# Reordered pairs, an earlier third softmax, stores by tile and sums zeroed by GpSimd in a four-layer graph network on one core

## The chip, the cores and the metric

The kernel runs on one core of one Trainium2 chip, as one program. The metric is the time of one execution in microseconds (us), as the device reports it. Beside it stands one execution taken by the hardware profiler, whose trace tells what each engine did: PE is the matrix engine, DVE the vector engine, ACT the scalar engine, POOL is GpSimd, SP the engine that here only issues transfers.

## The reference

The graph has 3125 nodes with rows of 256 numbers, and 53125 edges (50000 drawn ones and one loop per node), sorted by destination. Four layers follow each other, each with a residual and a layer norm. Cut to what matters:

```python
x = layernorm(x + gat_two_heads(x))        # e = exp(-leaky_relu(s_l[src] + s_r[dst])), sums over src
x = layernorm(x + gru(sum_over_edges(x[src] + rel[type]), x))
x = layernorm(x + poincare(x))             # below
x = layernorm(x + conv(relu(conv(x, edge_attr)), edge_attr))   # two TransformerConv, 4 heads
# poincare:
h = dir(x @ W.T + b) * magnitude
scores = h[src] @ a_s + h[dst] @ a_t
ex = exp(scores - segment_max(scores, dst)[dst]);  w = ex / (segment_sum(ex, dst)[dst] + 1e-10)
hc = h + segment_sum(h[src] * w, dst)
p = tanh(|hc|) * hc / |hc|, cut to length 0.95
# conv:
alpha = (q[dst] * (k[src] + e)).sum / 8, softmax over dst; out = segment_sum((v[src] + e) * alpha, dst) + x @ Ws + bs
```

## The kernel before, in words

Nodes lie in 25 tiles of 128 (`NT`), treated in 5 groups of 5 tiles (`NG`, `GRP`). Edges lie in 440 tiles of 128 (`ET`): 220 pairs, 55 groups of 8 tiles (`NH`, `HB`), 28 batches of 16 tiles (`NBT`, `NB`). The phases run one after the other, with a barrier of all engines between them: `start_up` (integers of the edges, first projection), `aggregate0` and `finish0` (first layer), `aggregate1` and `finish1` (second), `project2`, `aggregate2` and `finish2` (third, and the projections q, k, v, skip of the first conv), `attend(1)`, `between` (end of the first conv and the projections of the second), `attend(2)`, `last_rows`.

All aggregations work alike. POOL gathers the 128 source rows of a tile by an indirect transfer into a ring of slots (40 in the third layer). ACT weighs the rows, and PE multiplies them by a one-hot matrix (`oh`, written by DVE for 8 tiles at a time) into one of 4 windows in PSUM. DVE adds the window to the block of `acc` to which the tile's destinations belong. `acc` holds 128x6800 numbers and is zeroed by a DVE instruction at the head of each aggregation.

The third and fourth layers need a softmax over edges that share a destination. `RunningSoftmax` does it for a batch of 16 tiles in parts 0 to 7 (`sm.pe`, `sm.dve`, `sm.act`): the scores are turned by PE, DVE runs a running maximum along them, small transposes carry the values at tile ends across (`ends`, `car`, `firsts`, `back`), ACT takes the exponential, and PE turns the weights back (`w_in`). The parts are a chain: each waits for the one before, on another engine. In `aggregate2` a slot of the program is a batch: step j of 8 holds part j of the softmax of batch b-1, the scatter of pair j of batch b-2 on PE, and its windows' additions on DVE. So a pair is scattered 16 pairs after its scores. In `attend` the order is written by pairs p = 0, 1, ...: two parts of the softmax per pair in the first four pairs of every eight, none in the next four, and the scatter 12 pairs behind (`LAG`). Engines take their instructions strictly in the order written; POOL may refill a slot once the scatter of its old rows is done (`products`).

`finish2` has these chains per group of 5 tiles: DVE `combine(i)` writes hc; ACT squares it and takes the root of the sums; DVE `squash` asks ACT for a tanh (`t_ask`), works through twelve small instructions, five on rows and the moments; ACT takes a root; DVE `norm`; ACT writes the group's rows of `X`. Then PE transposes each tile, ACT copies it (`take_turned`), PE multiplies by the 256x1024 weights, and DVE takes the products (`take`, 4 instructions). `store` writes a whole group's k, v and skip rows by two transfers; the phase ends when all have landed. `between` has the same projection behind `rest(i)`, which ends the first conv, and `last_rows` writes the output.

Of the kernel before, what the change touches and what calls it, by code (L numbers as in the profile page):

```python
# [60 lines left out]
def graph_layers(nc, a, out):  # L61
    ctx = ExitStack()
    with ctx:
# [115 lines left out]
        def start_up():  # L179
# [6 lines left out]
            with ExitStack() as scope:  # L186
# [28 lines left out]
                with nc.Block() as block:  # L215
# [29 lines left out]
                    def _(pool):  # L245
# [8 lines left out]
                        nc.gpsimd.memset(ones[:, :], 1.0).then_inc(consts, 1)  # L254
                        pool.wait_ge(starts_ready, 1)
# [194 lines left out]
        def aggregate0():  # L450
            names = "lo_in0 lo_in1 lo_in2 lo_in3 oht_ready oh_ready z_terms z_ready w_ready rows_ready products added zeroed dve act".split()
            lo_in0, lo_in1, lo_in2, lo_in3, oht_ready, oh_ready, z_terms, z_ready, w_ready, rows_ready, products, added, zeroed, dv, ac = [
# [11 lines left out]
            with ExitStack() as scope:  # L464
# [5 lines left out]
                with nc.Block() as block:  # L470
# [45 lines left out]
                    def _(dve):  # L516
# [59 lines left out]
                        nc.vector.memset(acc[:, :, :], 0.0).then_inc(zeroed, 1)  # L576
# [3 lines left out]
                        dve.wait_ge(zeroed, 1)  # L580
# [48 lines left out]
        def finish0():  # L629
# [3 lines left out]
            with ExitStack() as scope:  # L633
# [4 lines left out]
                wprod = held(scope, "wprod2", [P, 2, F])  # L638
                rows = held(scope, "rows_f0", [P, 3, GRP, F])
                low = held(scope, "low_f0", [P, 2, GRP, F])  # L640
                with nc.Block() as block:
                    @block.vector
                    def _(dve):
# [31 lines left out]
                        dve.wait_ge(wt_taken, 10)  # L675
                        dve.wait_ge(ld_x, 16 * 8)
                        for n in range(2):
                            step(nc.vector.tensor_tensor(wprod[:, :, :], w2T[:, :, 0:F], bc_a2[:, n, :].unsqueeze(1).broadcast_to([P, 2, F]), ALU.mult))
                            step(nc.vector.tensor_reduce(w2T[:, :, F + 1 + n:F + 2 + n].rearrange("p k a -> p (k a)"), wprod[:, :, :], AX, ALU.add))
                            step(nc.vector.tensor_tensor(wprod[:, 0, :], bc_b2[:, 0:F], bc_a2[:, n, :], ALU.mult))  # L680
                            step(nc.vector.tensor_reduce(bc_b2[:, F + 1 + n:F + 2 + n], wprod[:, 0, :], AX, ALU.add))
                        step(nc.vector.tensor_tensor(bc_t[:, 0:512], bc_t[:, 0:512], bc_b[:, 0:512], ALU.add))
# [70 lines left out]
        def aggregate1():  # L753
            a_in = [sem(f"a1_a_in{u}") for u in range(2)]
            aT_out = [sem(f"a1_aT_out{u}") for u in range(2)]
            names = "oh_ready products added zeroed at_ready at_taken fix_in fix_out".split()
# [386 lines left out]
        def tiles_of(b):  # L1143
            return max(0, min(NB, ET - b * NB)) if 0 <= b < NBT else 0
# [353 lines left out]
        def finish2():  # L1498
            h_ready, n_ready, t_ask, t_ready, var_ready, std_ready, f_ready, x_ready, x_out, dv, ac = [
                sem("f2_" + n) for n in "h_ready n_ready t_ask t_ready var_ready std_ready f_ready x_ready x_out dve act".split()]  # L1500
            with ExitStack() as scope:
# [4 lines left out]
                with nc.Block() as block:  # L1506
                    @block.vector
                    def _(dve):
# [508 lines left out]
```

## Time and profile before

| | us |
|---|---|
| three timed runs | 4553.05, 4554.0, 4560.82 |
| median | 4554.0 |
| the profiled execution | 4529.55 |
| its span, first to last instruction | 4527.8 |
| PE busy in the span | 3176.2 (70%) |
| DVE busy | 2951.7 (65%) |
| POOL busy | 2749.4 (61%) |
| ACT busy | 1634.9 (36%) |

The profiled execution is 24.45 us below the median of the timed ones. Busy time is time with an instruction of the engine under way; no engine is near 100%, since each phase has another limit. The mean granted clock of PE is 0.806 of full speed. POOL's time is nearly all that of issuing indirect transfers.

### The profile page before, as it was taken

The numbers are of one execution on the slowest core, as the hardware profiler recorded it, in microseconds if no ns is written. First come the engines' busy times: TensorE is split into PE (matmuls) and PEld (weight loads), VectorE is DVE, ScalarE is ACT, GpSimd is POOL, SyncE is SP. The second block draws the span as 40 slices with busy tenths as digits, with TensorE's granted clock in tenths as the row PEclk, the third lists the DMA queues.
The fourth block names the chain that finished last, engine by engine and source line by source line (L and its number), as shares of the span: only waits on it lengthen the run. The fifth ranks groups of instructions, "written<-read, shape, count | busy, mean of one in ns | idle before, by whom it ended". The sixth has DMA issues, their size and how long they took to land. (4 is left out here: it accounts for less than half of the span.)

```text
span 4527.8 us, 51805 instructions
## 1 busy us (share of the span) xinstructions
PE 3176.2 (70%) x11623; PEld 2181.9 (48%) x11623; DVE 2951.7 (65%) x7240; ACT 1634.9 (36%) x4707; POOL 2749.4 (61%) x2215
## 2 busy tenths in 40 slices
PE   4555553476666853777775788888887878888884
PEld 3444442344444442444443356666564456666662
DVE  3445447344444464666665478888887578888887
ACT  3334444011111221223233245555552145555553
POOL 4666661766665005667760188888881288888881
PEclk7667776688887875556667889999998999999996
DMA  4544443566566203444441599999994599999993
GB/s 134 112 113 111 114 112 84 154 195 198 184 192 183 87 12 116 114 114 113 114 99 52 145 188 192 190 186 191 190 181 107 162 185 192 190 190 186 191 179 85
DMA packets 378970, 660.99 MB, mean 146 GB/s; under 512 B 59010, under 2 KB 161395, under 8 KB 378676
## 3 DMA queue, kind: packets, MB, share of 16 engines
q0 software_dynamic: 190208, 406.78, 47.5%
q1 hardware_dynamic: 184356, 247.08, 17.0%
q10 hardware_dynamic: 4112, 3.83, 0.3%
q8 instruction: 110, 1.80, 0.2%
q14 instruction: 184, 1.51, 0.1%
HBM read 582.15 MB, written 75.33 MB: 145 GB/s over the span
## 5 line engine op out<-in xcount | busy, mean ns | idle before, releaser
L1653 POOL DMA_INDIRECT t_kv<-kv_tab,srcT x880 | 1415.7, 1609 | 648.8 <-ACT t_kv L1779 389.4
L1280 POOL DMA_INDIRECT grow<-h_tab,srcT x440 | 451.2, 1025 | 468.3 <-POOLq L83 276.7
L776 POOL DMA_INDIRECT grow<-x_tab,srcT x440 | 441.1, 1003 | 304.2 <-issue 107.1
L1836 PE MATMUL bank<-t_kv,t_oh 128*128 128x260 f32 x1760 | 555.4, 418 | 99.8 <-DVE acc L1730 66.6
L476 POOL DMA_INDIRECT grow<-h_tab,srcT x440 | 436.2, 991 | 245.2 <-issue 96.6
L1809 PE MATMUL bank<-we,t_aT 128*128 128x256 f32 x1760 | 504.7, 413 | 26.2 <-DMA t_aT<-attrT_tab 25.5
L1820 PE MATMUL bank<-H,t_ohT 128*128 x1760 | 497.4, 409 | 23.0 <-DVE t_ks L1690 22.3
L1778 ACT COPY t_kv<-bank 128x512 f32<-128x512 f32 x440 | 256.3, 582 | 618.6 <-PE bank L1809 583.7
L1796 ACT ACTIVATE t_kv<-t_kv 128x64 f32<-128x64 f32 x1760 | 465.8, 344 | 13.4 <-DVE t_kv L1706 13.4
L824 DVE TENSOR_TENSOR acc<-acc,bank 128x272 f32 x440 | 192.5, 437 | 393.9 <-PE bank L901 151.3
L1836 PEld LDWEIGHTS bank<-t_kv,t_oh 128*128 128x128 f32 x1760 | 318.2, 201 | 258.5 <-ACT t_kv L1796 133.5
L1730 DVE TENSOR_TENSOR acc<-acc,bank 128x260 f32 x880 | 368.6, 419 | 98.3 <-DVE acc L1730 71.2
L1408 PE MATMUL bank<-grow,oh 128*128 128x257 f32 x880 | 393.8, 601 | 35.0 <-DVE acc L1337 16.1
L1820 PEld LDWEIGHTS bank<-H,t_ohT 128*128 128x128 f32 x1760 | 361.4, 207 | 88.3 <-issue 31.4
L901 PE MATMUL bank<-grow,oh 128*128 128x272 f32 x880 | 296.6, 462 | 121.9 <-issue 98.1
L1809 PEld LDWEIGHTS bank<-we,t_aT 128*128 128x128 f32 x1760 | 335.0, 200 | 81.6 <-DMA t_aT<-attrT_tab 27.2
L548 DVE TENSOR_TENSOR acc<-acc,bank 128x258 f32 x440 | 186.6, 424 | 274.7 <-PE bank L626 108.7
L626 PE MATMUL bank<-grow,oh 128*128 128x258 f32 x880 | 319.5, 535 | 37.0 <-issue 27.9
L1690 DVE TENSOR_TENSOR t_ks<-t_kv,bank 128x512 f32<-128x512 f32 x440 | 298.9, 679 | 68.8 <-DMA t_kv<-kv_tab,srcT 61.3
L1337 DVE TENSOR_TENSOR acc<-acc,bank 128x257 f32 x440 | 184.2, 419 | 192.4 <-PE bank L1408 135.1
L849 ACT COPY aT<-bank 128x512 f32<-128x512 f32 x110 | 64.1, 585 | 620.3 <-PE bank L874 285.7
L1408 PEld LDWEIGHTS bank<-grow,oh 128*128 128x128 f32 x880 | 236.9, 294 | 101.8 <-issue 41.7
(396 smaller groups left out, 4804.5 us busy)
## 6 DMA issues: line engine op xcount, KB each, us to landing
t_aT<-attrT_tab SPq DMA_DIRECT2D x110, 512.0 KB
lob<-lo_tab SPq DMA_DIRECT2D x110, 256.0 KB
arow<-in_edge_attr SPq DMA_DIRECT2D x440, 64.0 KB
attrT_tab<-aT SPq DMA_DIRECT2D x55, 512.0 KB
t_lob<-lo_tab SPq DMA_DIRECT2D x110, 256.0 KB
grow<-h_tab,srcT POOLq DMA_INDIRECT x880
t_kv<-kv_tab,srcT POOLq DMA_INDIRECT x880
kv_tab<-kv SPq DMA_DIRECT2D x10, 1290.0 KB, 5.2
```

The source lines that it names most:

```text
L476: nc.gpsimd.indirect_dma_start(out=grow[:, t % RA, :], out_offset=None, in_=h_tab, in_offset=bass.IndirectOffsetOnAxis(ap=srcT[:, t:t + 1] ...
L626: nc.tensor.matmul(PS[t % WIN][:, 0:F + 2], oh[:, g % 2, u, :], grow[:, t % RA, :], start=True, stop=True).then_inc(products, 1)
L776: nc.gpsimd.indirect_dma_start(out=grow[:, t % RA, 0:F], out_offset=None, in_=x_tab, in_offset=bass.IndirectOffsetOnAxis(ap=srcT[:, t:t + ...
L1280: nc.gpsimd.indirect_dma_start(out=grow[:, t % R2, :], out_offset=None, in_=h2_tab, in_offset=bass.IndirectOffsetOnAxis(ap=srcT[:, t:t + 1 ...
L1408: nc.tensor.matmul(PS[2 + t % WIN2][:, 0:F + 1], oh[:, t // HB % 2, t % HB, :], grow[:, t % R2, 0:F + 1], start=True, stop=True).then_inc( ...
L1653: nc.gpsimd.indirect_dma_start(out=kv[:, t % UB, :], out_offset=None, in_=kv_tab, in_offset=bass.IndirectOffsetOnAxis(ap=srcT[:, t:t + 1], ...
L1690: nc.vector.tensor_tensor(ks[:, p % 2, :, :], kv[:, s:s + 2, 0:F], PS[2 + p % 2][:, :].rearrange("p (v f) -> p v f", v=2), ALU.mult).then_ ...
L1730: nc.vector.tensor_tensor(window, window, PS[4 + t % WIN3][:, 0:LHW], ALU.add).then_inc(added, 1)
L1796: last = nc.scalar.activation(part, part, ACT.Copy, scale=u_rows[:, t % UB, h, C3:C3 + 1])
L1809: mm = nc.tensor.matmul(PS[p % 2][:, v * F:(v + 1) * F], aT[:, g % 3, u * P:(u + 1) * P], we[:, :], start=True, stop=True)
L1820: mm = nc.tensor.matmul(PS[2 + p % 2][:, v * F:(v + 1) * F], ohT[:, g % 2, u * P:(u + 1) * P], H[:, ds(blocks[u], 1), :].rearrange("p b f ...
L1836: nc.tensor.matmul(PS[4 + t % WIN3][:, 0:LHW], oh[:, t // HB % 2, t % HB, :], kv[:, t % UB, F:KVW], start=True, stop=True).then_inc(produc ...
```

## The change

The change has eight parts.

1. Zeroing `acc`. The DVE memset at the head of all five aggregations is gone. POOL zeroes the whole of it in `start_up`, and in `finish0`, `finish1`, `finish2` and `between` it zeroes each group's part (128x1360) once DVE has read it.
2. The score weights of the third layer (`wprod`, 8 instructions) go from the end of `finish0` to groups 10 and 12 of `aggregate1`; the addition to `bc_t` goes to the head of `aggregate1`.
3. `aggregate2` is written by pairs like `attend`: `LAG` 12, two parts of the softmax in each of the first four pairs of eight.
4. In both, the last batch's softmax is begun at pair 220 (`softmax_at`), in `attend` four pairs earlier than before, in `aggregate2` likewise as soon as its scores are there.
5. The last group's rows of the projections are stored tile by tile (`store_tiles`); the memset in `begin` covers only the columns that need it.
6. `finish2` puts `combine` and the squares of two groups ahead, and the chain of group i directly before that of i+1; the weights' `begin` comes one group later.
7. `between` puts `rest(i + 1)` behind the second `take` of group i.
8. `last_rows` stores the last group by tiles.

```diff
@@ start_up, POOL
                         nc.gpsimd.memset(ones[:, :], 1.0).then_inc(consts, 1)
+                        nc.gpsimd.memset(acc[:, :, :], 0.0)
@@ finish0, finish1, finish2, between: a POOL program like this one
+                            pool.wait_ge(h_ready, i + 1)
+                            nc.gpsimd.memset(group(acc, i), 0.0).then_inc(acc_zero, 1)
@@ aggregate2
+        LAG = 12
+        def softmax_at(p):
+            b, k = (p // 8 - 1, p % 8) if p < PAIRS else (NBT - 1, p - PAIRS)
+            return (b, k) if b >= 0 and k < 4 else None
@@ aggregate2, DVE
-                        nc.vector.memset(acc[:, :, :], 0.0)
...
-                        for b in range(NSLOT):
...
+                        for p in range(STEPS):
+                            q, batch = p - LAG, softmax_at(p)
+                            if batch:
+                                sm.dve(dve, step, batch[0], 2 * batch[1])
...
+                            if batch:
+                                sm.dve(dve, step, batch[0], 2 * batch[1] + 1)
+                                if batch[1] == 3:
+                                    take_weights(batch[0])
@@ Projection
+            def store_tiles(self, sp, i, tab):
+                for t in range(i * GRP, (i + 1) * GRP):
+                    sp.wait_ge(self.mm_taken, 2 * (t + 1))
+                    sp.dma_start(kv_tab[t * P:(t + 1) * P, :], self.kv[:, i % 2, t % GRP, :]).then_inc(self.out_done[i % 2], 16)
+                    sp.dma_start(tab[t * P:(t + 1) * P, :], self.skip[:, i % 2, t % GRP, :]).then_inc(self.out_done[i % 2], 16)
@@ finish2, DVE
+                        combine(0)
+                        combine(1)
                         for i in range(NG + 2):
                             if i < NG:
-                                combine(i)
-                            if i == 0:
-                                pr.begin(dve, step)
+                                squash(i)
                             takes(i - 2, 0, 2)
-                            if 1 <= i <= NG:
-                                squash(i - 1)
-                            takes(i - 2, 2, 3)
-                            if 1 <= i <= NG:
-                                norm(i - 1)
-                            takes(i - 2, 3, GRP)
+                            if i < NG:
+                                norm(i)
+                            if i + 2 < NG:
+                                combine(i + 2)
+                            if i == 1:
+                                pr.begin(dve, step)
+                            takes(i - 2, 2, GRP)
@@ between, DVE
-                            if i + 1 < NG:
-                                rest(i + 1)
                             add_bias(i)
-                            for t in range(i * GRP, (i + 1) * GRP):
-                                pr.take(dve, t)
+                            for n in range(GRP):
+                                pr.take(dve, i * GRP + n)
+                                if n == 1 and i + 1 < NG:
+                                    rest(i + 1)
```

PE in the middle of `aggregate2` before, from the end of one batch to the first four parts of the next softmax. L1408 is the scatter (two rows are a pair), L1185, L1188 and L1191 are the turned scores, the ends and the carried values of the softmax:

```order
L1408 MATMUL bank<-grow,oh 128x257 x4
L1185 MATMUL bank<-ident,s_al 16x128
L1408 MATMUL bank<-grow,oh 128x257 x2
L1188 MATMUL bank<-ident,s_run 1x16
L1408 MATMUL bank<-grow,oh 128x257 x2
L1191 MATMUL bank<-ident,s_rowC 16x1
L148 TENSOR_LOAD rows_i
```

The same place after; the scatter is now L1426, and the softmax L1205 to L1217:

```order
L1426 MATMUL bank<-grow,oh 128x257 x4
L1205 MATMUL bank<-ident,s_al 16x128
L1208 MATMUL bank<-ident,s_run 1x16
L1426 MATMUL bank<-grow,oh 128x257 x2
L1211 MATMUL bank<-ident,s_rowC 16x1
L1214 MATMUL bank<-ident,s_tot 1x16
L1426 MATMUL bank<-grow,oh 128x257 x2
L1217 MATMUL bank<-ident,s_rowC 16x1
L148 TENSOR_LOAD rows_i
```

Two small transposes that wait for each other through DVE now stand next to each other, with no scatter between, and the four pairs behind them have none.

ACT in `finish2` before, from the norm of group 1 on. L1578 and L1580 are the squares and their root, L1585 the tanh, L1588 the deviation's root, L1592 the rows of `X`, L1467 the copies of transposed tiles:

```order
L1580 ACTIVATE small<-ss 128x5
L1585 ACT_TABLE_LOAD
L1585 ACTIVATE small<-small 128x5
L1588 ACT_TABLE_LOAD
L1588 ACTIVATE small<-small 128x5
L1592 ACTIVATE X<-hc,small 128x256 x5
L1467 COPY xT<-bank 128x256 x2
L1578 ACTIVATE sq,ss<-hc 128x256 x5
L1580 ACTIVATE small<-ss 128x5
L1467 COPY xT<-bank 128x256
```

After, from the rows of `X` of group 0 on (L1610 and L1612 are the squares and root, L1620 the tanh, L1624 the deviation's root, L1629 `X`, L1492 the copies):

```order
L1629 ACTIVATE X<-hc,small 128x256 x5
L1610 ACTIVATE sq,ss<-hc 128x256 x5
L1612 ACTIVATE small<-ss 128x5
L1620 ACT_TABLE_LOAD
L1620 ACTIVATE small<-small 128x5
L1624 ACT_TABLE_LOAD
L1624 ACTIVATE small<-small 128x5
L1629 ACTIVATE X<-hc,small 128x256 x5
L1610 ACTIVATE sq,ss<-hc 128x256 x5
L1612 ACTIVATE small<-ss 128x5
L1492 COPY xT<-bank 128x256 x2
```

The first copies of transposed tiles, for which PE's first products wait, stood directly behind the first `X`; they now stand behind the second `X` and one more group of squares.

## Rows read from the trace of the kernel before

**Rows 1.** Windows of three phases: us, busy and count by engine, PEclk, DMA share, GB/s.
```profile
1728.00:2412.00 684.00, 476.39 (x1600) 307.05 (x1600) 414.28 (x1281) 193.24 (x496) 450.54 (x440) 0.61 0.41 107
2412.00:2572.00 160.00, 102.54 (x250) 46.19 (x250) 82.64 (x280) 48.63 (x126) 0.00 (x0) 0.82 0.27 95
2572.00:3468.00 896.00, 732.74 (x2920) 535.75 (x2920) 763.81 (x1804) 458.69 (x1377) 708.02 (x440) 0.94 0.97 179
```

**Rows 2.** The gathers of aggregate2 by source line: ns min/median/max; idle us, times.
```profile
L1280 POOL DMA_INDIRECT grow<-h_tab,srcT x440: 940/946/2226, 1727.4 to 2369.2; - x147
...
  issue: 109.5, 348
  PE bank L1408: 73.4, 84
```

**Rows 3.** PE groups of aggregate2: busy us, mean ns, idle before by releaser.
```profile
L1408 PE MATMUL bank<-grow,oh 128*128 128x257 f32 x880 | 393.8, 601 | 35.0 <-DVE acc L1337 16.1 <-ACT grow L1377 11.0 <-issue 7.6
```

**Rows 4.** Timeline of aggregate2: start us, us, engine, line, [idle before <-releaser].
```profile
1749.69 0.17 DVE L1313 TENSOR_TENSOR s_al<-s_al,grow 128x8 f32<-128x8 f32 x1 [7.87 <-DMA grow<-h_tab,srcT]
...
1773.79 0.16 DVE L1321 COPY s_fm<-bank 128x1 f32<-128x1 f32 x1 [11.88 <-remote]
...
2349.69 0.14 DVE L1230 COPY s_carry<-bank 16x1 f32<-16x1 f32 x1
...
2350.93 0.41 DVE L1235 TENSOR_TENSOR_SCAN s_tot<-contn,s_T 16x128 f32<-16x128 bf16 x1
...
2351.50 2.08 PE L1408 MATMUL bank<-grow,oh 128*128 128x257 f32 x4
...
2372.44 1.11 PE L1408 MATMUL bank<-grow,oh 128*128 128x257 f32 x4
...
2376.38 0.17 DVE L1313 TENSOR_TENSOR s_al<-s_al,grow 128x8 f32<-128x8 f32 x1
...
2410.56 0.42 DVE L1337 TENSOR_TENSOR acc<-acc,bank 128x257 f32 x1 [0.21 <-DVE acc L1337]
```

**Rows 5.** Timeline at the head of aggregate2, DVE.
```profile
1728.19 5.72 DVE L1339 MEMSET acc<- 128x6800 f32 x1 [5.44 <-issue]
...
1741.04 0.17 DVE L1313 TENSOR_TENSOR s_al<-s_al,grow 128x8 f32<-128x8 f32 x1 [4.88 <-DMA grow<-h_tab,srcT]
```

**Rows 6.** Timeline of finish2: ACT, then PE and DVE.
```profile
2417.85 0.21 ACT L1580 ACTIVATE small<-ss 128x5 f32<-128x5 f32 x1
...
2431.36 0.21 ACT L1585 ACTIVATE small<-small 128x5 f32<-128x5 f32 x1
...
2437.86 0.21 ACT L1588 ACTIVATE small<-small 128x5 f32<-128x5 f32 x1 [4.99 <-DVE small L427]
...
2442.39 5.25 PE L1459 MATMUL bank<-wq,xT 128*128 128x512 f32 x8
...
2445.96 0.42 DVE L1484 SCALAR_TENSOR_TENSOR H<-bank,b_all 128x256 f32<-128x256 f32 x1 [5.07 <-PE bank L1459]
...
2449.62 0.43 DVE L1484 SCALAR_TENSOR_TENSOR H<-bank,b_all 128x256 f32<-128x256 f32 x1 [1.18 <-PE bank L1459]
...
2462.99 0.69 PE L1448 MATMUL bank<-ident,X 128*128 128x128 f32 x2 [4.38 <-ACT X L1592]
```

**Rows 7.** Timeline at the ends of finish2 and last_rows: last takes, next phase, last store.
```profile
2561.72 0.41 DVE L1490 TENSOR_TENSOR skip<-bank,b_all 128x256 f32<-128x256 f32 x1
...
2570.41 0.35 SPq L1662 DMA_DIRECT2D t_aT<-attrT_tab  x1
...
4521.37 0.41 SPq L1953 DMA_DIRECT2D out_nodes<-H  x1
```

**Rows 8.** Timeline of DVE in start_up and at the end of finish0.
```profile
4.39 0.38 DVE L274 TENSOR_SCALAR blk_of_edge_i<-I 128x420 int32<-128x420 int32 x1 [1.49 <-DMA I<-in_dst]
...
785.88 0.69 DVE L678 TENSOR_TENSOR wprod<-w2T,bc_a 128x512 f32<-128x512 f32 x1
...
790.60 0.69 DVE L682 TENSOR_TENSOR bc_t<-bc_t,bc_b 128x512 f32<-128x512 f32 x1
```

More of the change, by code:

```diff
@@ L928, in finish1, with _ @@
                 u_rows = held(scope, "u_f1", [P, GRP, F])
+                acc_zero = sem("f1_acc_zero")
                 with nc.Block() as block:
+                    @block.gpsimd
+                    def _(pool):
+                        for i in range(NG):
+                            pool.wait_ge(xt_ready, (i + 1) * GRP)
+                            nc.gpsimd.memset(group(acc, i), 0.0).then_inc(acc_zero, 1)
                     @block.sync
@@ new lines, in _ @@
+                        for p in range(STEPS):
+                            q, batch = p - LAG, softmax_at(p)
+                            if batch:
+                                sm.pe(pe, batch[0], 2 * batch[1], sums_done, min(NH, 2 * batch[0] + 2))
+                            if p % 4 == 2 and p // 4 < NH:
+                                terms(p // 4)
+                            if batch:
+                                sm.pe(pe, batch[0], 2 * batch[1] + 1, sums_done, 0)
+                            if 0 <= q < PAIRS:
+                                for t in range(2 * q, 2 * q + 2):
+                                    if t % HB == 0:
+                                        pe.wait_ge(oh_ready, t // HB + 1)
+                                    pe.wait_ge(rows_ready, t + 1)
+                                    if t >= WIN2:
+                                        pe.wait_ge(added, t - WIN2 + 1)
+                                    nc.tensor.matmul(PS[2 + t % WIN2][:, 0:F + 1], oh[:, t // HB % 2, t % HB, :], grow[:, t % R2, 0:F + 1],
+                                                     start=True, stop=True).then_inc(products, 1)
@@ L1505, in finish2, with _ @@
                 pr = Projection(scope, 1, X, None)
+                acc_zero = sem("f2_acc_zero")
                 with nc.Block() as block:
+                    @block.gpsimd
+                    def _(pool):
+                        for i in range(NG):
+                            pool.wait_ge(h_ready, i + 1)
+                            nc.gpsimd.memset(group(acc, i), 0.0).then_inc(acc_zero, 1)
                     @block.vector
@@ L1572, in copies, with squares @@
                                 pr.take_turned(act, t)
+                        def squares(i):
+                            act.wait_ge(h_ready, i + 1)
+                            for n in range(GRP):
+                                last = nc.scalar.activation(sq[:, n, :], hc[:, i % 3, n, :], ACT.Square, accum_out=ss[:, i % 3, n:n + 1])
+                            step(last)
+                            nc.scalar.activation(small[:, i % 3, 4, :], ss[:, i % 3, :], ACT.Sqrt).then_inc(n_ready, 1)
@@ L1580, in _ @@
[L1580 to L1592 removed]
+                                act.wait_ge(t_ask, i + 1)
@@ L1875, in between, with _ @@
                 pr = Projection(scope, 2, H, xr)
+                acc_zero = sem("b_acc_zero")
                 with nc.Block() as block:
+                    @block.gpsimd
+                    def _(pool):
+                        for i in range(NG):
+                            pool.wait_ge(h_ready, i + 1)
+                            nc.gpsimd.memset(group(acc, i), 0.0).then_inc(acc_zero, 1)
                     @block.sync
```

245 lines of the change are left out of this document (111 added, 134 removed).

## The prediction

> **What bounds the kernel now.** I read the page first. No engine is near its limit over the whole span, so the question is asked phase by phase, with a window each [rows 1]. In `attend` the DMA engines are busy 0.97 of the time at a PE clock of 0.94, for 896 us: whatever is taken off DVE there is behind transfers. In `aggregate2` (684 us) nobody is full: PE 476 of 684, DVE 414, POOL 451, DMA 0.41, and PE's granted clock is 0.61, so it is most of the time at its lower level of 1.2 GHz. In `finish2` (160 us) PE is busy 102.5, and idle for the rest.
>
> For `aggregate2` I then read who waits. POOL's shortest path is its gathers: 0.95 us each, and 0.31 (109.5/348) between two that wait for nothing; 73.4 us went by waiting for PE to free a ring slot [rows 2]. So the order of PE's work holds POOL up. The first batch of 16 tiles is scored at 1749.7 and the last, half a batch, at 2376.4 [rows 4]: 626.7 us over 26.5 batches, **23.65 us a batch**. POOL alone would need 16 x 1.26 = 20.2. Of PE, a pair of scatters is 1.11 us at its higher clock and 2.08 at its lower [rows 4]. The group's sum, 393.8 us over 220 pairs, is 1.79 a pair [rows 3], which lies between.
>
> In `finish2` the chain of group 0 runs 24.5 us from the root at 2417.9 to PE's first product at 2442.4; tiles then follow at a pitch of 2449.62 - 2445.96 = 3.66 us, until PE has to wait for the next group's `X`, 4.38 us at 2463.0 [rows 6]. From 2442.4 to the last take at 2562.1 it is 119.7 us [rows 6, 7], where the first tile's 5.25 and 24 x 3.66 would be 93.1.
>
> **`aggregate2`, new order.** The half of a batch with the softmax (four pairs) and the free half are costed apart. Softmax half on PE, at the low clock: 4 x 2.08 = 8.3 for scatters. All that PE does besides scatters in this window is 476.4 - 393.8 = 82.6 us [rows 1, 3], 3.0 a batch, of which the half has the larger part, 2.2. Then the waits of transposes that now stand side by side. The worst is from `car` to `tot`: DVE's chain from 2349.69 to 2351.34 [rows 4] is 1.65, and with the way there and back some 2.2; the two before and behind it I put at 1.1 each, by the length of their shorter chains on DVE. Sum 8.3 + 2.2 + 4.4 = **14.9**. Free half: at the low clock PE would need 8.3 + 0.8 = 9.1; at the high one 4.4 + 0.6, and DVE becomes the bound with 8 additions at a pitch of 0.42 + 0.21 = 0.63 [rows 4], 5.0, and some 2.1 for one-hots, places and scores (DVE's 414 us of work [rows 1] are 15 a batch, of which additions 6.7, softmax about 4.7, and the rest 3.6 is halved): 7.1. So a batch costs between 14.9 + 7.1 = 22.0 and 14.9 + 9.1 = 24.0. I take 22.1, since PE had pairs of 1.11 us in a third of the time already, and the free half lets it run without gaps. That is 1.55 x 26.5 = 41 us. Bounds: if PE were at the high clock throughout, POOL's 16 x (1.025 busy [451/440, rows 1] + 0.31) = 21.3 is next, a gain of 62; at the low clock throughout and with waits a little longer (24.3), a loss of 17.
>
> The tail: from the last scores, 2376.4, to the last addition's end, 2411.0, it is 34.6 us [rows 4]. The new tail has one softmax half (14.9, without terms 14), then 8 pairs at DVE's pitch of 2 x 0.63 = 1.27 (10.2) and some 5 for last waits: 29, so **5** gained (0 to 9). The ring: a slot comes free 12 instead of 16 pairs after its scores, so POOL's lead grows by 8 tiles; this takes the 73.4 us of waiting away and is in the 22.1 already.
>
> **`finish2`.** New chain from the squares on: root of group 0 at 2418.1 as now; squares of group 1 end 2.2 later, 2420.3; the tanh with its table 1.6 later; from tanh to the deviation's root 2437.86 - 2431.36 = 6.5 [rows 6], 2428.4; `X` of group 0 done at 2431.5. Squares(2) to 2433.8, tanh(1) 2435.3, root 2441.8, `X` of group 1 at 2444.9, squares(3) 2447.2, and only now the first copies: PE starts at **2447.7**, 5.3 later than now. But then two groups of `X` lie ready, and each further group (about 13.4 us of ACT and DVE chain) is due within 18.3 us (5 x 3.66) of PE's: PE runs without gaps, 93.1 us, to 2540.8, plus 1.2 for the last take, 2542. Against 2562.1 that is 20 (15, if one stall of 4.4 stays, to 21).
>
> **Stores by tile.** From the last take to the next phase's first transfer it is 2570.41 - 2562.13 = 8.3 us, for 1.98 MB [rows 7]. The output's last group, 0.6 MB, needs 6.4 from its issue to the span's end. By these two a MB costs 1.4 us and one tile (0.40 MB) 6.1; a steeper slope cannot be excluded, with a fixed part of 3.5 it would be 4.5. Gain 2.2 to 3.8, taken **3** in `finish2` and **3** in `between`; for `last_rows` 0.5 to 2.5, taken 1.
>
> **Zeroing.** At the head of `aggregate2` DVE's 5.72 us end at 1733.9, and its first scores wait another 4.88 us, until 1741.0, for a gather [rows 5]: worth 0 there, and as the gathers start with the phase in every aggregation, in all five. On POOL, 20 memsets of a group are at DVE's speed 5.72/5 = 1.14 us each, in phases where POOL has no gather [rows 1]: 0 if hidden, 23 if each delayed DVE by its length; taken 1 lost. In `start_up` the whole memset starts at about 2.1 and ends at 7.8; DVE wants to begin at 4.39 [rows 8]. Lost between 0 and 3.4, and more if POOL is slower than DVE; taken **3**.
>
> The Trainium skill, "SBUF — State Buffer", section "Who interferes with whom", says that a DVE instruction in a two-port mode and a GpSimd instruction exclude each other for the whole instruction, and one with at most one SBUF input outside such modes doesn't contend. No row of the trace shows such an overlap. By that rule the start would lose the 3.4, and the group memsets only what meets a copy or a scalar operation.
>
> **The rest.** In `attend` the last batch's softmax begins four pairs earlier; DMA ends the phase at 0.97, and in the tail DVE and PE have room: 1.5 each, together 3 (0 to 6). `finish0` sheds nine DVE instructions, 785.88 to 791.29, 5.4 us [rows 8], but the store of `x_tab` issued just ahead has to land: 2 (0 to 5). They come back in `aggregate1`, twice 2.2 us between additions, where DVE has idle time: 0 (-4 to +4). `rest(i + 1)` behind the takes in `between`: 0.
>
> Sum: 41 + 5 + 20 + 3 + 3 + 1 + 3 + 2 - 3 - 1 = **74**. The profiled execution would go from 4529.6 to 4456 and the median, 24 above it, from 4554 to **4480**.
>
> **Rivals.** (A) *The clock stays low in `aggregate2`.* For it: 0.61 now, and waits added in the softmax half. 24.3 us a batch is 17 lost instead of 41 gained: 4480 + 58 = 4538. With 24.0 it is 4530. Against: PE's idle gaps in the free half go. Chance 0.15. (B) *Slower than before.* At 1773.79 DVE waited 11.88 us [rows 4] for something that the profile doesn't name, while POOL filled the ring at its full rate. In the new order POOL is never held, so such stalls could recur all along; in one of every four batches they cost 7 x 12 = 84 us and cancel the 74 with the 9 us more that 0.2% is. From 7 on the kernel is slower; 10 would give 4600. Against: in `attend` POOL is busy 708 of 896 us and PE as much [rows 1] without such gaps. Chance 0.05.
>
> The Trainium skill, "Runtime: NRT & Kernel Launch", section "Instruction fetch mechanics", says that instructions are fetched in sequence and mostly hidden, and that a taken branch can stall an engine. By this rule such a stall belongs to a phase's head and would not recur; B would then be worth nothing.
>
> (C) *POOL's own pace is reached*: 21.3 a batch, 21 us more gained, 4459. For it: DVE and PE both have room at the high clock. Chance 0.14. (D) *GpSimd's memsets shut DVE out* in all phases: 22 more lost, 4502. It decides nothing alone. Chance 0.04. (E) *Nothing measurable*: A together with stalls left in `finish2`, or a first gather later by what POOL has before it; 4546 to 4563. Chance 0.04.
>
> **How the numbers follow.** The main case has 0.58 and gives 4480; its own range, from the bounds of its terms taken two or three at a time, is 4462 to 4504. The range for all reaches to C below and A above: **4448 to 4538**, which leaves out B, E and the edges of A, some 1.5 in 10. 0.2% is 9 us, about what this measurement can tell from no change. Main, A, C and D are faster by more (0.91, less 0.02 for A at its worst); B is slower 0.05, E gives the same 0.04 and the rest of A 0.02. So 0.89, 0.06, 0.05.
>
> **What would show it.** In the profile after: `aggregate2` some 640 us with a granted clock above 0.61, POOL's waits for PE nearly gone, batches 22 us apart; `finish2` about 137 us, its first product later by 5 us and no wait of PE for `X`; 5 us from the last take to the next phase; in `start_up` DVE's first instruction on the integers at 7.8. The forecast is wrong if a batch takes 24 us, at a clock of 0.55, or if each second pair in the softmax half waits longer than 2.2.

## The result, and the profile after

The changed kernel takes 4540.5 us (median of 9 runs, 4520.3 to 4544.9) where the kernel before takes 4553.1 (9 runs on the same chip, 4546.9 to 4566.9): ratio **0.9967**, 95% interval 0.9952 to 0.9981. It is faster, by 13 us by the medians and 15 by the ratio, and not by 74. The predicted 4480 was missed, and the range of 4448 to 4538 too, by 2.5 us. The profiled execution is, against that, 13 us longer than the one before (span 4540.9 against 4527.8). Two single profiles 0.3% apart don't decide on the whole, but they show where the stages moved.

The first view has the windows, one each for `aggregate2`, `finish2`, `attend(1)` and `between` (columns as in [rows 1]):

```profile
1739.00:2453.00 714.00, 445.59 (x1600) 302.45 (x1600) 415.60 (x1279) 194.38 (x497) 439.76 (x440) 0.63 0.39 102
2453.00:2587.00 134.00, 94.70 (x250) 43.53 (x250) 80.86 (x279) 48.78 (x126) 6.24 (x5) 0.84 0.32 112
2587.00:3487.00 900.00, 737.46 (x2920) 538.39 (x2920) 757.76 (x1806) 458.59 (x1377) 710.72 (x440) 0.93 0.97 178
3487.00:3598.00 111.00, 94.87 (x250) 43.45 (x250) 66.46 (x154) 9.32 (x25) 6.16 (x5) 0.93 0.49 165
```

`finish2` fell from 158.6 to 134 us, as forecast. `aggregate2`, which was to give 46 us, grew from 685 to 714, with a granted clock that did rise (0.61 to 0.63) and PE 31 us less busy. The gathers of that phase by source line, to be set beside [rows 2]:

```profile
L1300 POOL DMA_INDIRECT grow<-h_tab,srcT x440: 940/946/1733, 1739.6 to 2405.3; - x147
...
  PE bank L1426: 104.5, 88
  issue: 102.8, 323
```

POOL waits longer for PE than before (104.5 us after 73.4), in spite of the eight slots more of lead. Of each of these waits (84 before, 88 now) 0.30 us is the pause that stands between any two gathers. One batch in the timeline of that trace (start us, us, engine, line; the scatter is L1426, the turned scores L1205, the turned weights L1223):

```profile
1898.30 0.28 PE L1205 MATMUL bank<-ident,s_al 128*16 128x128 f32 x1 [2.50 <-DVE s_al L1333]
...
1901.49 0.17 PE L1211 MATMUL bank<-ident,s_rowC 1*16 1x1 f32 x1
1901.89 0.15 DVE L1250 COPY s_carry<-bank 16x1 f32<-16x1 f32 x1 [0.90 <-PE bank L1211]
...
1905.90 0.17 PE L1217 MATMUL bank<-ident,s_rowC 1*16 1x1 f32 x1
1908.26 0.15 DVE L1272 COPY s_carry<-bank 16x1 f32<-16x1 f32 x1 [2.41 <-DMA flags<-f_tab]
...
1910.02 2.08 PE L1426 MATMUL bank<-grow,oh 128*128 128x257 f32 x4 [2.12 <-issue]
...
1912.91 0.26 PE L1223 MATMUL bank<-ident,s_d 16*128 16x16 f32 x1
...
1914.47 0.42 DVE L1357 TENSOR_TENSOR acc<-acc,bank 128x257 f32 x1 [1.03 <-PE bank L1426]
...
1916.17 0.43 DVE L1349 TENSOR_TENSOR acc<-acc,s_fm 128x257 f32 x1 [0.42 <-issue]
...
1922.70 0.28 PE L1205 MATMUL bank<-ident,s_al 128*16 128x128 f32 x1 [2.52 <-DVE s_al L1333]
```

The batch takes 24.4 us: 14.6 with the softmax, to the turned weights, and 9.8 without. DVE gets the second carried value (L1272) 2.36 us after the start of the transpose that makes it (L1217), a transpose of 16 numbers; over the batches the mean of this is 1.3 us. Over batches 4 to 24 the mean period is 24.4 us, worked out from the starts of L1205: 14.1 to the turned weights and 10.3 behind them.

`finish2` went by its forecast steps. Its ACT and PE rows after, beside [rows 6], with the last take and the next phase's first transfer, beside [rows 7]:

```profile
2462.71 0.21 ACT L1620 ACTIVATE small<-small 128x5 f32<-128x5 f32 x1
2469.21 0.21 ACT L1624 ACTIVATE small<-small 128x5 f32<-128x5 f32 x1 [4.99 <-DVE small L428]
...
2487.74 0.21 ACT L1612 ACTIVATE small<-ss 128x5 f32<-128x5 f32 x1
2488.35 6.11 PE L1484 MATMUL bank<-wq,xT 128*128 128x512 f32 x8 [14.74 <-ACT xT L1492]
...
2494.51 3.60 PE L1484 MATMUL bank<-wq,xT 128*128 128x512 f32 x8
...
2582.32 0.41 DVE L1515 TENSOR_TENSOR skip<-bank,b_all 128x256 f32<-128x256 f32 x1
...
2587.40 0.34 SPq L1697 DMA_DIRECT2D t_aT<-attrT_tab  x1
```

The tanh-to-root chain is 6.5 us again; PE starts 35.4 us into the stage instead of 30.5 (4.9 later, forecast 5.3) and needs 94.4 us to the last take (forecast 94.3). From there it is 4.7 us to the next transfer where it was 8.3.

### The profile page after: what moved, and what is told of

Its sections match the earlier page's. It is cut to its first block and busy times, and to the rows that moved or that the text cites. A ratio compares the mean times of both kernels' runs of the same rounds, so it can differ in the third digit from the quotient of the medians.

```text
span 4540.9 us, 51843 instructions
## 1 busy us (share of the span) xinstructions
PE 3139.2 (69%) x11623; PEld 2176.7 (48%) x11623; DVE 2928.8 (64%) x7235; ACT 1634.8 (36%) x4707; POOL 2766.9 (61%) x2236
## 5 line engine op out<-in xcount | busy, mean ns | idle before, releaser
L1300 POOL DMA_INDIRECT grow<-h_tab,srcT x440 | 439.8, 999 | 313.4 <-PE bank L1426 104.5
L477 POOL DMA_INDIRECT grow<-h_tab,srcT x440 | 432.2, 982 | 256.7 <-issue 95.4
L822 DVE TENSOR_TENSOR acc<-acc,bank 128x272 f32 x440 | 192.5, 438 | 405.1 <-PE bank L907 180.2
L1426 PE MATMUL bank<-grow,oh 128*128 128x257 f32 x880 | 359.8, 566 | 54.7 <-ACT grow L1397 32.5
L907 PE MATMUL bank<-grow,oh 128*128 128x272 f32 x880 | 299.1, 467 | 98.7 <-issue 62.5
L625 PEld LDWEIGHTS bank<-grow,oh 128*128 128x128 f32 x880 | 233.4, 275 | 107.7 <-issue 41.8
L1426 PEld LDWEIGHTS bank<-grow,oh 128*128 128x128 f32 x880 | 228.3, 279 | 111.1 <-issue 47.5
```

What stands on the lines that cost most here:

```text
L477: nc.gpsimd.indirect_dma_start(out=grow[:, t % RA, :], out_offset=None, in_=h_tab, in_offset=bass.IndirectOffsetOnAxis(ap=srcT[:, t:t + 1] ...
L625: nc.tensor.matmul(PS[t % WIN][:, 0:F + 2], oh[:, g % 2, u, :], grow[:, t % RA, :], start=True, stop=True).then_inc(products, 1)
L907: nc.tensor.matmul(PS[t % WIN1][:, 0:AC], oh[:, g % 2, u, :], grow[:, t % RA, :], start=True, stop=True).then_inc(products, 1)
L1300: nc.gpsimd.indirect_dma_start(out=grow[:, t % R2, :], out_offset=None, in_=h2_tab, in_offset=bass.IndirectOffsetOnAxis(ap=srcT[:, t:t + 1 ...
L1426: nc.tensor.matmul(PS[2 + t % WIN2][:, 0:F + 1], oh[:, t // HB % 2, t % HB, :], grow[:, t % R2, 0:F + 1], start=True, stop=True).then_inc( ...
```

## The experiments

Each ran beside the kernel before on one chip. The chips were of two kinds: on four of them the kernel before takes 4302 to 4309 us, here the faster kind; three times, the first measurement among them, it took 4522 to 4554, the slower kind. The first two traces are of the slower kind. Each chip was used in one sitting only, so "kind" is a name for what was seen: whether it belongs to the chip for good is not shown. A stage's length is that in the one profiled execution of its run.

**1. The old order of `aggregate2` in the changed kernel.** The phase is that of before, without DVE's memset.

```diff
-                        for p in range(STEPS):
-                            q, batch = p - LAG, softmax_at(p)
+                        for b in range(NSLOT):
+                            c = b - 2
+                            for j in range(8):
```

> The changed kernel with one part undone: aggregate2 has the order of before (a batch's softmax over eight pairs, scatter 16 pairs behind), without the memset on DVE. Theory 1, read from the trace after: the new order made aggregate2 longer, 24.4 us a batch instead of 23.4, because its two halves are bound in turn by the softmax's chain (14.3 us) and by DVE's own chain (9.8 us); undoing it takes 27 us off the changed kernel, some 4513 us or 0.991 of the kernel before, and the stage is back at some 685 us. Rival: the stage lost because the clock of PE fell in that one profiled execution; then the time stays at 4540, 0.997. Second rival: zeroing by GpSimd disturbed the stage; then it stays long here too, at some 714 us.

4264.5 us against 4304.3, ratio 0.9905 (0.9890 to 0.9921), `aggregate2` 626.5 us. The ratio is the expected one by chance: the chip was of the faster kind. The stage was 60 us shorter than in the trace before with the same order, and so were `aggregate0` (597 for 676) and `aggregate1` (596 for 689). The rest of the change is worth 40 us there.

**2. The new order alone**, in the kernel before.

> The kernel before with one part of the change alone: aggregate2's new order, LAG 12 and the last batch's softmax begun early; the memset on DVE stays. Theory 1: slower than before by 27 us, some 4580 us or 1.006, with a stage of some 712 us. If the clock was to blame, 1.000. By the prediction on record it would be 0.990.

0.9961 (0.9947 to 0.9974), stage 606.4 us: 20 us less than the old order, where theory 1 wanted more. So the order is not longer by its own chains on every chip; this one is of the faster kind.

**3. One-hot matrices moved** out of the half without softmax:

```diff
-                            if g >= 2:
-                                dve.wait_ge(products, (g - 1) * HB)
+                            if g >= 3:
+                                dve.wait_ge(products, (g - 2) * HB)
...
+                            if p % 8 == 2 and 0 < (q + 6) // 4 < NH:
+                                one_hots((q + 6) // 4)
                             if batch:
                                 sm.dve(dve, step, batch[0], 2 * batch[1])
```

> The changed kernel with the one-hot matrices of the second group of a batch (1.22 us of DVE) moved out of the half without softmax into the place where DVE waits 1.36 us for the transposed values; this needs a third buffer for them, nothing else. Theory 1: the free half is DVE's chain, so it shrinks from 9.8 to 8.6 us and the softmax half keeps its 14.3: 23.2 us a batch, 32 us off the stage, some 4508 us or 0.990 of before. Rival: PE at its granted clock sets the free half; then the batch stays at 24.4 us and the ratio at 0.997.

The changed kernel with this has 0.9908 (0.9892 to 0.9923) and a stage of 624.5 us, 18 more than without it. On this kind of chip DVE's wait for the transposed value was 0.26 us and not 1.36. The softmax half grew from 11.6 to 12.5 us, and the half that lost 1.22 us of DVE's work shrank by 0.2 only. The account behind experiment 9 shows what the 18 us are: longer gathers.

**4. `finish2`'s order alone**, in the kernel before.

> The kernel before with one part of the change alone: finish2's new order on DVE and ACT (stores by group, no zeroing on GpSimd). By the prediction on record PE starts 5 us later and then never waits for X: 20 us gained, 4533 us or 0.9956, stage some 139 us instead of 158.6. Rival: only the stores by tile and the stage's end gained, and PE's waits only moved: ratio 0.999 and over.

0.9955 (0.9941 to 0.9968), 4282.9 against 4304.3: 21 us, stage 137.5 after 158.6. The step stands.

**5. The changed kernel once more.**

> The changed kernel itself once more, beside the parts. Theory 2, formed from the first four runs: they ran on a chip whose kernel before takes 4304 us instead of 4554; there aggregate2's new order gained 17 us instead of losing 29, and PE's results came 0.87 us after their start where in the first two traces they came some 4 us later in stretches of full granted clock. If the cause of the miss is that slower PE, the sum of the parts holds on such a chip: 4304 - 41 (all but aggregate2) - 18 = some 4245, ratio 0.986. Rival: the parts don't add up (the one-hot variant had 0.9908), ratio 0.991. If the chip is again of the slower kind, 0.997.

4246.3 us against 4303.9, **0.9856** (0.9840 to 0.9873), `aggregate2` 605.9 us. The parts add up, and on this chip the whole gained 58 us by the medians. Repeated twice, both times on the faster kind:

> The changed kernel once more, for a second profile and ratio on a chip of the slower kind, if this is one (kernel before over 4500 us). There theory 2 expects aggregate2 at some 710 us, 27 us over the old order's 684 in the run before this, and a ratio of 0.997 to 0.9985; on the faster kind 606 us and 0.986.

> The changed kernel beside its variant with the old aggregate2, on one chip. If the chip is of the slower kind: 0.997 with the stage at some 712 us. On the faster kind 0.986 and 606 us.

0.9859 (0.9842 to 0.9875) and 0.9869 (0.9851 to 0.9888), stage 604.1 in the latter. Beside it the old order on the same chip:

> The changed kernel with aggregate2 in the old order, on the same chip as the run before it. Slower kind: 0.991 to 0.994, stage 684 us, so 0.3% to 0.6% faster than the changed kernel there. Faster kind: 0.9905, 0.5% slower than it.

0.9914 (0.9898 to 0.9929), stage 627.6. The one-hot variant came out as in experiment 3, twice: 0.9906 (0.9890 to 0.9923), stage 621.4, and 0.9902 (0.9888 to 0.9916), stage 631.5.

> The changed kernel with the second group's one-hot matrices written where DVE waits for the transposed values. On the faster kind of chip that wait was only 0.26 us, and the stage became 18 us longer. On the slower kind the wait is 1.36 us, as long as the instruction: there it hides, and the free half loses 1.2 us: stage some 33 us under the changed kernel's 714, at 681. Rival: PE's late results set the free half too, and the stage stays at 714. On the faster kind: 624 us and 0.9908 again.

> The changed kernel with the one-hot matrices moved into DVE's wait. Slower kind: some 690 us for the stage and 0.992, if DVE's chain bounds the free half; 714 and 0.997 if late results of PE do. Faster kind: 624 us, 0.9907.

On the slower kind this variant was not measured, so its question there stays unanswered.

**6. Zeroing alone**, in the kernel before: GpSimd's memsets in five phases, DVE's gone.

> The kernel before with the zeroing part of the change alone: GpSimd zeroes the sums in start_up and by groups in four phases, DVE's five memsets are gone. By the prediction on record 4 us are lost (3 in start_up, 1 by the groups), since the memsets lay under the wait for the first gathers: 1.001. Rival: the memsets did cost their 5.7 us at each of the five heads and 25 us are gained net, 0.995.

0.9981 (0.9972 to 0.9991): 8 us gained, where 4 lost were forecast. `start_up` is 2 to 3.5 us longer, but `aggregate1` 588.8 us after 596 to 598 on the same kind of chip. Its gathers, in this kernel's trace by source line:

```profile
L782 POOL DMA_INDIRECT grow<-x_tab,srcT x440: 942/946/1985, 722.3 to 1293.5; - x147
```

The longest is 1.99 us, and the first takes 1.44. In the traces with DVE's memset at that head the longest, the first, takes 8.46 us. On the faster kind POOL never waits in this stage (below), so that the 7 us come off it whole. With `start_up` that makes 4 to 5 of the 8 us; the interval allows 4 to 12. In the ten traces of that kind without the memset the stage is 589 to 596 us; those of the changed kernel also have the score weights in it.

**7. The zeroing of `start_up` later**, behind GpSimd's transfers:

```diff
-                        nc.gpsimd.memset(acc[:, :, :], 0.0)
                         pool.wait_ge(starts_ready, 1)
                         pool.wait_ge(pk_out, 48)
                         for j in range(J):
                             nc.gpsimd.indirect_dma_start(...)
+                        nc.gpsimd.memset(acc[:, :, :], 0.0)
```

> The changed kernel with GpSimd's zeroing of all sums in start_up behind the indirect transfers that it issues there, instead of ahead of them. In the trace after, DVE's first instruction on the integers took 3.56 us instead of 0.38 and ended when the memset did. Theory: start_up is 4 us shorter, 59.3 instead of 63.4 us, and the rest stays: 0.999 of the changed kernel. Rival: DVE is held later by as much, and start_up stays at 63.

> The changed kernel with GpSimd's zeroing of start_up behind the transfers it issues there: start_up 60.4 us instead of 63.6 on either kind of chip, so 3 us off the time, 0.9993 of the changed kernel.

`start_up` is 60.4 and 59.8 us where the changed kernel has 63.8 and 63.3 on the same chips, so the 3.5 us are there. The whole is too noisy to show them: 0.9871 (0.9853 to 0.9888) beside 0.9856 on one chip, 0.9953 (0.9936 to 0.9971) beside 0.9966 on another. DVE's first instruction on the integers in the trace after, and GpSimd's memset:

```profile
4.48 3.56 DVE L275 TENSOR_SCALAR blk_of_edge_i<-I 128x420 int32<-128x420 int32 x1 [1.58 <-DMA I<-in_dst]
...
2.06 5.76 POOL L255 MEMSET acc<- 128x6800 f32 x1
```

The instruction took 0.38 us before [rows 8]. It now ends at 8.04, just behind the memset (7.82), and with the memset moved it is back:

```profile
4.47 0.38 DVE L275 TENSOR_SCALAR blk_of_edge_i<-I 128x420 int32<-128x420 int32 x1 [1.56 <-DMA I<-in_dst]
```

**8. PE given double work in `aggregate2`**, in either order: each scatter is issued twice, and the second writes the same numbers again.

```diff
+    nc.tensor.matmul(PS[2 + t % WIN2][:, 0:F + 1], oh[...], grow[...], start=True, stop=True)
     nc.tensor.matmul(PS[2 + t % WIN2][:, 0:F + 1], oh[...], grow[...], start=True, stop=True).then_inc(products, 1)
```

> A kernel that makes PE slow on purpose in aggregate2 alone: each scatter matmul is issued twice (the second overwrites the first with the same numbers), so a pair costs PE twice its time. The rest is the changed kernel, aggregate2 in the order of before. Theory 2: where PE's real rate in the scatters is low, the order that spreads the softmax over eight pairs loses less. Doubled work of 393.8 us spread over the batch: stage some 800 us, 29 us a batch. Rival: PE fills its idle time at the higher clock, and the stage stays under 700.

> The same doubling with aggregate2 in the new order, so the changed kernel with each scatter matmul of that phase issued twice. Theory 2: the stage is longer than that of the old order with the same doubling, by 1 to 2 us a batch (30 to 50 us), where without doubling it was 20 us shorter. Rival: the new order keeps its 20 us, or more, when PE has twice the work; then a slow PE doesn't explain the loss on the first chip.

> The changed kernel with aggregate2 in the order of before, once more, in case the chip is of the slower kind of the first two traces (kernel before at 4554 us). There: stage at some 685 us instead of 714, 4513 us, ratio 0.991, so faster than the changed kernel's 0.997. On the faster kind: 0.9905 again, behind the changed kernel's 0.9856.

This chip was of the slower kind (before 4522). Old order with doubling: 0.9978 (0.9959 to 0.9996), stage 698.5 us, granted clock 0.91. New order with doubling: 1.0205 (1.0177 to 1.0233; two executions only), stage 814.1 us, clock 0.76. Old order without: 0.9940 (0.9919 to 0.9961), 683.6 us, clock 0.60. The size for the old order was expected wrongly (800): doubled work costs it 15 us, with PE at its higher level for most of the stage. The new order is 116 us longer under the same load. POOL's pauses in it add up to 333 us, after 207 in the old order. That PE stands while two transposes wait for DVE, and then has less time for more work, is my reading of the order and was not tested by itself.

**9. Both orders on one chip of the slower kind.**

> The changed kernel beside the two below on one chip. Slower kind of chip: 0.997, aggregate2 some 712 us. Faster kind: 0.986, 606 us.

> The changed kernel with aggregate2 in the old order. Slower kind: 0.991 to 0.994, stage 684 us. Faster kind: 0.991, stage 626 us.

The changed kernel 4527.4 us, 0.9966 (0.9949 to 0.9984), stage 703.2; with the old order 4510.1 us, **0.9923** (0.9904 to 0.9941), stage 687.1. On one and the same chip the new order costs 16 us of its stage, where on the faster kind it gains 20 to 23. The changed kernel of experiment 7 on this chip has 702.8.

**Where the stage's time goes, by POOL's rows.** POOL does nothing in `aggregate2` but its 440 gathers. Their lengths, the pauses between them, the time behind the last and 0.7 us ahead of the first add up to the stage:

| `aggregate2`, us | old order | new order | one-hots moved | old order | new order |
|---|---|---|---|---|---|
| kind, experiment | faster, 5 | faster, 5 | faster, 5 | slower, 9 | slower, 9 |
| stage | 627.6 | 604.1 | 631.5 | 687.1 | 703.2 |
| gathers | 449.5 | 433.4 | 459.6 | 446.8 | 437.4 |
| pauses | 133.7 | 133.8 | 133.8 | 199.6 | 218.5 |
| behind the last | 43.8 | 36.3 | 37.3 | 40.1 | 46.7 |

The rows of the three on the faster kind, which share a chip (old, new, one-hots moved; L83 is the time ahead of the phase):

```profile
L1305 POOL DMA_INDIRECT grow<-h_tab,srcT x440 | 449.5, 1022 | 221.5 <-issue 95.6 <-POOLq L83 87.7 <-PE bank L1432 38.1
L1300 POOL DMA_INDIRECT grow<-h_tab,srcT x440 | 433.4, 985 | 221.3 <-issue 91.7 <-POOLq L83 87.5 <-PE bank L1426 42.1
L1300 POOL DMA_INDIRECT grow<-h_tab,srcT x440 | 459.6, 1045 | 221.9 <-issue 94.8 <-POOLq L83 88.1 <-PE bank L1428 39.0
```

On the faster kind all 439 pauses are the 0.30 us of a gather that waits for nothing, in every one of its twelve traces and in either order. POOL never waits there: it sets the stage, and an order can shorten it only by shorter gathers or a shorter tail. The gathers differ by where they meet DVE's one-hot instruction. In the old order (first three rows, experiment 5) one begun 0.14 us into it takes 1.88 us; in the new one (last three) the instruction begins just behind a gather, and the next meets only its end:

```profile
1858.01 1.21 DVE L1328 TENSOR_TENSOR oh<-iota_n,dlocT 128x1024 f32<-128x1024 f32 x1
1858.15 1.88 POOL L1305 DMA_INDIRECT grow<-h_tab,srcT  x1 [0.30 <-issue]
1860.34 0.95 POOL L1305 DMA_INDIRECT grow<-h_tab,srcT  x1 [0.30 <-PE bank L1432]
...
1858.80 0.95 POOL L1300 DMA_INDIRECT grow<-h_tab,srcT  x1 [0.30 <-issue]
1858.93 1.22 DVE L1323 TENSOR_TENSOR oh<-iota_n,dlocT 128x1024 f32<-128x1024 f32 x1
1860.05 0.95 POOL L1300 DMA_INDIRECT grow<-h_tab,srcT  x1 [0.31 <-issue]
```

Of the 52 gathers begun inside that instruction in the old order 50 take over 1.0 us, 32 us above 0.946 each in sum. In the new order it is 31 of 54, with 10 us. With the one-hots moved it is 35 of 35, with 17.5 us, and the gathers still under way when it begins have 22.5 more. On the slower kind the pauses come to 66 and 85 us more than 0.30 each, and it is this waiting for PE that the new order lengthens.

## Why the prediction was wrong

| us | forecast | faster kind | slower kind |
|---|---|---|---|
| kernel before | | 4302 to 4309 | 4522 to 4554 |
| `aggregate2`, order and tail | -46 | -20 to -23 | +16 (+29 in the first two traces) |
| `finish2`, order | -20 | -21 | -24 for both |
| `finish2`, stores by tile | -3 | -3.4 | in the row above |
| `between` | -3 | -4 | -4 |
| `last_rows` | -1 | -0.7 | -0.7 |
| `finish0` | -2 | -2.8 | -2.8 |
| `start_up` | +3 | +3.5 | +4 |
| `aggregate1` | 0 | -8 (zeroing alone) | not told apart |
| `attend`, both | -3 | not told apart | not told apart |
| whole | -74 | -56 to -62 | -15 to -16 |

**The step that failed** is the cost of a batch in the new `aggregate2`, "So a batch costs between 14.9 + 7.1 = 22.0 and 14.9 + 9.1 = 24.0. I take 22.1". Measured by the starts of L1205 it was 24.4 us in the trace after and 24.0 in that of experiment 9. The 2.3 us over the forecast are 61 us of the stage, which is the miss. Of the two halves it was the free one. I put it at 7.1 us, DVE's additions, one-hots, places and scores, and took PE's 9.1 at the low clock for the unlikely bound. Its mean was 10.3 and 11.0 us on the slower kind, and 9.1 on the faster. The rows of the batch above show some of what was left out: DVE waits 1.03 us for the first product, since ACT can weigh no row until the weights are there, the first additions come at a wider pitch than 0.63, and `rescale` (L1349) takes 0.43 with a wait of 0.42. The batch on the faster kind, below, has the same three, so they don't explain the difference between the kinds. The softmax half, put at 14.9, had a mean of 14.1 and 13.0 on the slower kind and 11.6 on the faster.

So rival A's price came (24.3 us a batch, 4538), but not its reason: the granted clock rose. That the two agree is luck.

**The premise that failed** stands ahead of that sum: "So the order of PE's work holds POOL up." On the faster kind nothing holds POOL up, in the old order either. Its batch there is 21.3 us, which is the price that the forecast gave to "POOL's own pace" (rival C), and the new one is 20.7, since the gathers are shorter (0.985 us in the mean after 1.022). The 62 us that rival C counts from 23.65 down to it don't exist on such a chip. The gain of 20 to 23 us there comes from shorter gathers (16 us in experiment 5) and a shorter tail (7), the first of them for no reason that the forecast has. Where the one-hots fall against the gathers was no part of its plan, so these 16 us are luck. On the slower kind POOL does wait beyond its pauses, 58 us before. The forecast read 73.4, with the pauses in them, and let the new order take them away; the 58 became 93.

**The slower kind of chip.** The same kernel's batch on the faster kind, in the timeline of a trace of experiment 5:

```profile
1850.19 0.28 PE L1205 MATMUL bank<-ident,s_al 128*16 128x128 f32 x1 [1.70 <-DVE s_al L1333]
...
1852.60 0.17 PE L1211 MATMUL bank<-ident,s_rowC 1*16 1x1 f32 x1 [0.39 <-DVE s_rowC L1246]
1852.87 0.15 DVE L1250 COPY s_carry<-bank 16x1 f32<-16x1 f32 x1 [0.27 <-PE bank L1211]
...
1856.88 0.17 PE L1217 MATMUL bank<-ident,s_rowC 1*16 1x1 f32 x1
1857.08 0.15 DVE L1272 COPY s_carry<-bank 16x1 f32<-16x1 f32 x1 [0.26 <-PE bank L1217]
...
1861.73 0.26 PE L1223 MATMUL bank<-ident,s_d 16*128 16x16 f32 x1
...
1870.70 0.28 PE L1205 MATMUL bank<-ident,s_al 128*16 128x128 f32 x1 [1.70 <-DVE s_al L1333]
```

The value of L1217 reaches DVE in 0.20 us here, against 2.36. DVE's and ACT's instructions have the same lengths in both; what differs is when PE's results come. The two carried values are only a part of it. They come 1.7 us a batch later in the trace after than here, of 3.7 us that the batch is longer, but 0.9 of 3.3 on the slower chip of experiment 9. The additions wait for their products longer as well: 137 and 155 us over the stage, against 95. The effect shows best in `aggregate1`, which the order doesn't touch. PE's busy time there is nearly the same (448 and 441 us) and so is POOL's (443 and 444), yet the stage is 698 us after 594. From a chip of the slower kind (the changed kernel of experiment 9), PE's scatter is L907 and DVE's addition L822:

```profile
927.40 2.65 PE L907 MATMUL bank<-grow,oh 128*128 128x272 f32 x8 [0.63 <-DVE acc L822]
...
932.27 0.44 DVE L822 TENSOR_TENSOR acc<-acc,bank 128x272 f32 x1 [3.06 <-DMA x_tab<-X]
...
932.86 0.70 PE L907 MATMUL bank<-grow,oh 128*128 128x272 f32 x2 [2.37 <-issue]
933.73 0.44 DVE L822 TENSOR_TENSOR acc<-acc,bank 128x272 f32 x1 [1.02 <-issue]
```

PE's first tile of these four starts at 927.40 and DVE gets it at 932.27, 4.9 us later, with a granted clock of 1.0 in this stretch. I took all additions in `aggregate1` for which DVE waited over 0.5 us, with the clock at 1.0 from the tile's start to DVE's. The median of that way is 0.87 us in every trace of the faster kind and 3.4 to 3.7 in those of the slower. In those it grows with the time since the clock rose, counted to DVE's start and over all eight traces: 1.0 us in the first two, 3.4 from the fourth to the sixth, 5.0 from the twelfth on. With the clock at 0.5 throughout it is 1.4 on the faster kind and 1.3 to 1.4 in seven of the eight traces of the slower, by only 4 to 11 additions each. In the first four after a fall it is 6 to 8 there. So PE delivers late in stretches that the trace calls full, and its records, whose ends are modelled, hide it. A lateness that builds up speaks for PE working off less there than its records say, rather than for a longer way of each result; no run tests that. The granted clock in the stage is also lower, 0.78 to 0.81 against 0.86 to 0.89. Whether that is a cause or comes of PE standing more is not shown either. In `attend(1)` no difference is seen: 893 to 903 us on the faster kind, 894 to 902 on the slower. The forecast read one trace, of one kind of chip, and took its 23.65 us a batch as a property of the order: it was 21.3 on the other kind, by the spacing of the windows' additions.

**The steps that held**: `finish2` (start 4.9 us later, no further wait for `X`), stores by tile (3.6 us off the end), `between`, `finish0`, `start_up`. The tail of `aggregate2`, from the last scores to the last addition's end, was 34.6 us and came to 29.5: 5 gained, as forecast. On the faster kind it went from 35.2 to 27.8. Of the two-sided question at `start_up`, the rule of the Trainium skill, "SBUF — State Buffer", section "Who interferes with whom", is borne out by the row of 3.56 us: a DVE instruction of the kinds that the rule names was held to the end of GpSimd's memset, while the tensor-tensor instruction at 2.15 ran its 0.76 us as before. The group memsets, 1.23 to 1.25 us each, cost nothing visible: `finish0`, `finish2` and `between` are as short as forecast. The forecast's "worth 0 there" was carried from `aggregate2` to all five aggregations, and that was wrong for `aggregate1`. [Rows 5] are of `aggregate2`, where gathers ran undisturbed beside the memset. In `aggregate1` the first gather was held, 8.46 us, and in `aggregate0` the fourth, 3.86 us; both rows stood in the trace before, and the forecast's "No row of the trace shows such an overlap" passed over them. Which gather is held and which is not stays open.

**What stays open**: what makes PE late on the slower kind of chip, and how much of the 24.4 us a batch is due to it. Rival B's stall, 11.9 us before, came in the first batch after too, 12.7 us, and did not recur; in the traces of experiment 5 it is not there.

## What to carry to other kernels

Before an order of other engines is changed to free the one that gathers, take the number of its pauses and their sum: 439 pauses of 0.30 us mean that it waits for nothing, and only shorter gathers or a shorter tail will help. Look at long gathers for the instruction of DVE that stands beside them. A price that is read from one trace holds for that chip: the same order cost 23.4 us a batch on one and 21.3 on another, and 2 us a batch are more than the order was worth on either, so read two. When the idle half of a loop is costed from one engine's busy time, list the first wait of the half and every instruction that stands once in it. Doubling PE's work is a cheap test of an order's room: here one order lost 15 us to it on its chip, and the other was 111 us over its undoubled stage on another chip of the kind.

## What the runs showed of the hardware

- The same program takes 4302 to 4309 us on four chips and 4522 to 4554 in three other measurements, all of it in the three aggregations that gather rows (in `aggregate1` 589 to 598 against 673 to 699 us), none in `attend(1)`, `finish1` or `finish2`. On the first four POOL's pauses in these aggregations are 0.30 us throughout; in the others they come to 58 to 93 us more in each, doubled runs aside.
- A gather of 128 rows takes 0.95 us. Begun 0.14 us into a DVE tensor-tensor instruction of 1.21 us on 128x1024 numbers it takes 1.88.
- In the doubled old order PE's clock rose from 0.60 to 0.91, and twice the scatters cost 15 us.
- GpSimd zeroes 128x6800 numbers in 5.76 us (DVE: 5.72) and 128x1360 in 1.23 to 1.25.
- With DVE's memset at the head of `aggregate1`, GpSimd's first gather there takes 8.46 us, in the changed kernel 0.95.
